# Five stage borders reordered, and the layer 0 cross attention issued in pairs of key tiles, in a four-layer decoder kernel

## The reference

```python
xn = layer_norm(x, g1, b1)                  # the context, 2 x 77 rows
ln_lat = layer_norm(latents, g2, b2)        # x after its own LayerNorm, 2 x 1024 rows
q = ln_lat @ Wq                             # 16 heads of 64
k, v = split(concatenate([xn, ln_lat], axis=1) @ Wkv)
weight = where(full_mask, einsum('bhld,bhnd->bhln', q * scale, k * scale), neg)
out = softmax(weight) @ v                   # 1024 queries, 1024 + 77 keys per item and head
return out @ Wout

x = x + L0_attn(_layernorm(x))          # gated scan
x = x + L0_xattn(ctx_1024, _layernorm(x), ...)      # as above
x = x + L0_ffn(_layernorm(x))           # integer weights, 256 -> 1024 -> 256
x = x + L1_attn(_layernorm(x))          # linear attention with two decays
x = x + L1_xattn(ctx_1024, ctx_1024, _layernorm(x));  x = x + L1_ffn(_layernorm(x))   # 8 experts
x = x + L2_attn(_layernorm(x))          # linear attention: 16 heads of 16, LayerNorm behind it
x = x + L2_xattn(...);  x = x + L2_ffn(...);  x = x + L3_attn(...);  x = x + L3_xattn(...);  x = x + L3_ffn(...)
```

## Time and profile before

| | us |
|---|---|
| median of 3 runs | 3242.64 (3238.62 to 3245.68) |
| the profiled execution's own time | 3243.5 |
| its span in the trace | 3241.8 |
| PE busy | 2901.1 (89%) |
| DVE busy | 1949.8 (60%) |
| ACT busy | 1456.5 (45%) |
| POOL busy | 1210.1 (37%) |
| mean granted TensorE clock | 0.943 |

### The profile page before, as it was taken

How to read it: one execution, slowest core, us unless ns; L and a number is a source line. 1 busy time by engine, 2 the same in 40 slices (tenths; PEclk the granted TensorE clock), 3 DMA queues, 4 the chain that set the end, 5 groups by cost and what they waited for, 6 DMA issues and landing times. The chain is left out here.

```text
span 3241.8 us, 48893 instructions
## 1 busy us (share of the span) xinstructions
PE 2901.1 (89%) x18490; PEld 1956.2 (60%) x18490; DVE 1949.8 (60%) x3101; ACT 1456.5 (45%) x2394; POOL 1210.1 (37%) x1001
## 2 busy tenths in 40 slices
PE   7869999999999979999998695999687888899977
PEld 6745555555555548888884564999465565344355
DVE  6556676676676754224218774555447858666576
ACT  3334444444444434324324373777333635355664
POOL 0026666666666640000004341566133403122232
PEclk9979999999999989999998896999798999799989
DMA  1100000000000002111101005666300000000010
GB/s 59 49 7 1 1 1 1 1 1 1 1 1 1 1 19 62 46 33 59 46 14 33 22 2 181 205 202 195 71 1 16 5 10 1 2 1 1 1 33 27
DMA packets 117131, 114.51 MB, mean 35 GB/s; under 512 B 22827, under 2 KB 102726, under 8 KB 116902
## 3 DMA queue, kind: packets, MB, share of 16 engines
q1 hardware_dynamic: 103173, 97.66, 9.7%
q0 software_dynamic: 7488, 9.48, 1.6%
q10 hardware_dynamic: 6240, 4.26, 0.4%
HBM read 100.81 MB, written 11.47 MB: 35 GB/s over the span
## 5 line engine op out<-in xcount | busy, mean ns | idle before, releaser
L827 POOL TENSOR_TENSOR acc<-acc,pf 128x512 f32<-128x512 f32 (+1 forms) x448 | 570.8, 1297 | 206.7 <-ACT pf L952 206.7
L1009 DVE TENSOR_REDUCE mxa<-ps 128x1 f32<-128x512 f32 x512 | 329.3, 684 | 290.3 <-PE ps L873 290.0
L952 ACT ACTIVATE pf<-ps 128x512 f32<-128x512 f32 x512 | 277.9, 595 | 278.0 <-PE ps L848 253.7
L861 PE MATMUL ps<-pf,v 128*64 128x512 f32 (+1 forms) x1152 | 311.7, 620 | 0.0
L3737 ACT ACTIVATE pT<-ps 128x1024 f32<-128x1024 f32 (+1 forms) x192 | 154.1, 811 | 134.3 <-PE ps L3654 133.8
L1204 POOL TENSOR_TENSOR x<-x,ys 128x256 f32<-128x256 f32 x16 | 11.8, 739 | 510.5 <-DVE ys L1409 510.5
L3750 DVE TENSOR_REDUCE mx<-ps 128x2 f32<-128x1024 f32 (+1 forms) x192 | 175.1, 951 | 45.4 <-PE ps L3641 37.4
L1858 POOL TENSOR_TENSOR e<-e,sm 128x1232 f32<-128x1232 f32 x48 | 107.9, 2247 | 168.3 <-DVE sm L2128 168.3
L2588 DVE TENSOR_TENSOR w_lo<-w2a,w_hi 128x2048 fp32r<-128x2048 f32 x39 | 89.4, 2292 | 101.5 <-ACT w_hi L2475 101.5
L2387 PE MATMUL ps<-xT,w1r 128*128 128x128 f32 x1248 | 148.2, 278 | 0.0
L2387 PEld LDWEIGHTS ps<-xT,w1r 128*128 128x128 f32 x1248 | 144.9, 195 | 0.0
(11 more groups left out here) (550 smaller groups left out, 7380.5 us busy)
## 6 DMA issues: line engine op xcount, KB each, us to landing
w1r<-in_f_w SPq DMA_DIRECT2D x39, 1024.0 KB, 5.1
w_raw<-in_c_h SPq DMA_DIRECT2D x32, 512.0 KB, 4.3
w2a<-in_f_w SPq DMA_DIRECT2D x8, 1024.0 KB, 13.0
w_raw<-in_c_w SPq DMA_DIRECT2D x32, 128.0 KB, 2.3
x<-in_x SPq DMA_DIRECT2D x1, 2048.0 KB, 8.2
moe_rows<-rowbuf ACTq DMA_DIRECT2D x4, 512.0 KB, 8.2
moe_acc<-x ACTq DMA_DIRECT2D x1, 2048.0 KB, 9.5
x<-moe_acc SPq DMA_DIRECT2D x4, 512.0 KB, 5.5
```

Of the source, the lines that this page charges most:

```text
L827: pool.tensor_tensor(now[0:r, :], now[0:r, :], pf[0:r, n % RING, a, :], ALU.add).then_inc(added.sem, 1)
L861: ins = pe.matmul(g.bk(3)[SIDE[a], :], v[0:r, u // 2 % 2, t, u % 2 * P + a * HD:u % 2 * P + (a + 1) * HD], pf[0:r, n % RING, a, :], start= ...
L952: act.activation(pf[0:r, n % RING, a, :], g.bk(bk.bank[f"s{n}_{a}"])[0:r, :], ACT.Exp, bias=bias)\
L1009: dve.tensor_reduce(mxa[:, q % 2, half, a, j:j + 1], g.bk(4 + a), AXX, ALU.max).then_inc(bk.release(f"m{q}_{i}_{a}"), 1)
```

## The change

Six parts, cut to the core. In the profile of the changed kernel the lines of the cross attention read: scores L862 and L859, values L872, maxima L884 and L888, sums L899, turn L909, v L916, k and q L925; DVE maxima L1035, lower halves L1065, reciprocal L1079, negation L1049 to L1055. The tile ws there also names the room of the probabilities.

**Into the cross attention.** The attention stage loads the 12 weight blocks and makes wH; its tail makes the statistics of x tiles 0 to 11. ScalarE writes both zH and zf from PSUM; VectorE no longer rounds.

```diff
+                for grp in range(4):
+                    for i, src in enumerate(nsrc):
+                        load(sp, nraw[:, grp, i], rows(src[grp]), next_in[grp])
...
+                        if f == 2:
+                            act.wait_ge(*next_in[c].at(0, 16 * len(nsrc)))
+                            act.activation(nH[:, c], nraw[:, c], ACT.Copy).then_inc(nH_made.sem, 1)
+                for n in (2, 3):
+                    root_scalar(g, act, 0, EARLY, spread, rooted, n)
...
-                added(NC - 1)
+                dve.wait_ge(*bk.read(f"y1_{NC - 2}", 0))
+                rows_vector(g, dve, 0, EARLY, spread, link)
+                inverse_vector(g, dve, 0, EARLY, rooted, 2, link)
+                variance_twice(g, dve, 0, EARLY, spread, link)
+                added(NC - 1, (0,))
+                inverse_twice(g, dve, 0, EARLY, rooted, 3, link)
+                added(NC - 1, (1,))
...
+                    normal(range(0, TC))
+                    for t in range(EARLY, NT):
+                        dve.bn_stats(bn[:, t - EARLY, :], g.x[:, t, :])
+                    normal(range(TC, 2 * TC))
...
-                        act.activation(wH[:, grp], ws[:, grp], ACT.Copy).then_inc(wH_made.sem, 1)
+                            src, how = g.bk(bk.bank[f"t{k}_{c}"])[:, 0:w], dict(scale=cols[:, at, k:k + 1], bias=cols[:, at + 1, k:k + 1])
+                            act.activation(zH[:, k, c0:c0 + w], src, ACT.Identity, **how).then_inc(zH_made.sem, 1)
+                            act.activation(zf[:, k, c0:c0 + w], src, ACT.Identity, **how).then_inc(bk.release(f"t{k}_{c}"), 1)
+                        if c < 2:
+                            roots(c)
```

```diff
-        TURN_AT, SUMS_AT, SCALE_AT, Y_AT, REC_AT = 6, 1, 4, (5, 7), {2: (0, 1), 3: (2, 3)}
-        QUERY_AT, KEYS_AT = 0, {2: 0, 3: 1, 4: 2}
-        VALUES_AT = {(0, 2): 0, (0, 3): 1, (0, 4): 2, (1, 2): 3, (1, 3): 4}
+        TURN_AT, SUMS_AT, SCALE_AT, Y_AT, REC_AT = 5, 0, 4, (6, 8), {1: (0, 1), 2: (2,), 3: (3,)}
+        QUERY_AT, KEYS_AT = 2, {1: 0, 3: 1, 4: 2}
+        VALUES_AT = {(0, 1): 0, (0, 3): 1, (0, 4): 2, (1, 1): 3, (1, 3): 4}
         VALUE_STEPS = 5
         KCOLS = [(0, CH), (CH, CH), (S, LP)]
 
-        MAXIMA_AT = {0: (1, 2), 1: (1, 3), 2: (1, 4), 3: (1, 5), 4: (1, 6), 5: (1, 7), 6: (2, 8), 7: (2, 0), 8: (2, 1)}
-        NEGATED_AT = 5
+        MAXIMA_AT = {0: (1, 4), 1: (1, 6), 2: (1, 5), 3: (1, 7), 4: (2, 0), 5: (2, 2), 6: (2, 1), 7: (2, 3), 8: (2, 8)}
+        NEGATED_AT = 3
 
...
-        fills = [(misc[o], 6 + i % 2) for i, o in enumerate(others)]
-        fills += [(f"s{n}_{a}", (2 * n + a) % 3) for n in range(Q * NT9) for a in range(HN)] + [(f"o{q}", 3) for q in range(Q)]
-        fills += [(f"m{q}_{i}_{a}", 4 + a) for q, i in items for a in range(HN)]
+        fills = [(misc[o], i % 4 if i < len(opened + between) else 7) for i, o in enumerate(others)]
+        fills += [(f"s{n}_{a}", 2 * (n % 2) + a) for n in range(Q * NT9) for a in range(HN)] + [(f"o{q}", 4) for q in range(Q)]
+        fills += [(f"m{q}_{i}_{a}", 5 + a) for q, i in items for a in range(HN)]
         bk = Banks(g, fills)
...
+                for n in range(0, Q * NT9, 2):
+                    for k in (n + 2, n + 3):
+                        if k < Q * NT9:
+                            scores(k)
+                    for m in maxima_in(*divmod(n, NT9)):
                         maxima(*m)
+                    for o in others_in(*divmod(n, NT9)):
+                        other(*o)
                     values(n)
-                    for o in others_in(q, t):
+                    if n % NT9 != NK:
+                        values(n + 1)
+                    for o in others_in(*divmod(n + 1, NT9)):
                         other(*o)
+                    if n % NT9 == NK:
+                        values(n + 1)
+                    for m in maxima_in(*divmod(n + 1, NT9)):
+                        maxima(*m)
                 for o in tail:
...
-                    for m in maxima_in(q, t):
-                        maxima(*m)
-                    if n:
-                        for o in others_in(*divmod(n - 1, NT9)):
-                            other(*o)
+                    if n % 2 == 0:
+                        for m in maxima_in(q, t):
+                            maxima(*m)
+                    for o in others_in(q, t):
+                        other(*o)
+                    if n % 2:
+                        for m in maxima_in(q, t):
+                            maxima(*m)
```

```diff
+                dve.wait_ge(*bk.read(misc["y", Q - 2, 1], 0))
+                rows_vector(g, dve, 0, EARLY, spread, link)
                 for part in range(TC):
                     invert(Q - 1, part)
                 scale(Q - 1)
-                for o in tail:
+                for o in tail[:-1]:
                     other(*o)
+                inverse_vector(g, dve, 0, EARLY, rooted, 1, link)
+                other(*tail[-1])
                 link.close()
...
-        def load_first(sp):
-            for m in range(RAW):
-                block_load(sp, m)
-            for dst, src in ((c1, s1), (c2, s2), (c3, hs1), (c4, hs2), (r3, s3)):
-                load(sp, dst[:], src, c_in)
-
-        ln_block(g, load_first)
```

```diff
+                        if HT <= t <= EARLY + 1:
+                            done = range(2 * (t - HT), min(2 * (t - HT) + 2, EARLY))
+                            if done and t <= EARLY:
+                                moments(g, dve, done)
+                            if t == EARLY + 1:
+                                link(moments(g, dve, (10, 11)))
+                                variance_vector(g, dve, 0, EARLY, spread, link)
...
+                def shifts(a, b):
+                    dve.scalar_tensor_tensor(shift[:, a:b], g.mean[:, a:b], -1.0, g.rstd[:, a:b], ALU.mult, ALU.mult).then_inc(shift_made.sem, 1)
+
+                shifts(0, EARLY)
                 dve.wait_ge(*none_made.at(0, 2))
                 for i in range(NI):
                     ins = dve.tensor_copy(summed[:, i, i * NH:(i + 1) * NH], hs[:].rearrange("p (h d) -> p h d", d=HD)[:, :, 0])
```

```diff
-        DONE, LEFT, FINISH_AT = 8, 3, {12: (0, 1), 13: (2,), 14: (3,), 15: (4,), 16: (5,), 17: (6, 7)}
+        DONE, LEFT, FINISH_AT = 8, 3, {12: (0, 1), 13: (2, 3), 14: (4,), 15: (5,), 16: (6, 7)}
+        MOMENTS_AT = {14: (0, 1), 15: (2, 3), 16: (4, 5), 17: (6, 7)}
...
-                    sp.dma_start(brow[0:1, i, :].rearrange("o (f p) -> o f p", p=P), src.rearrange("p f -> f p").unsqueeze(0), allow_slow_non_contiguous=True)\
-                        .then_inc(b_in.sem, 16)
-                for dst, src in ((wk, Wk), (wq, Wq)):
-                    for k in range(KD):
-                        sp.dma_start(dst[:, k].rearrange("p (h d) -> p h d", d=HD),
-                                     rows(src)[:, k].rearrange("p (h e) -> p h e", e=2 * HD)[:, :, 0:HD]).then_inc(kq_in.sem, 16)
-                for dst, src in ((same, same_head), (cau, causal), (wv, rows(Wv)), (rv, bv), (wo, rows(Wo)), (ro, bo)):
+                    load(sp, bpad[:, i, :], src, b_in)
+                load(sp, wkr[:], rows(Wk), kq_in)
+                load(sp, wqr[:], rows(Wq), kq_in)
+                load(sp, same[:], same_head, b_in)
...
+                dve.wait_ge(*kq_in.at(0, 32))
+                for dst, src in ((wk, wkr), (wq, wqr)):
+                    dve.tensor_copy(dst[:].rearrange("p k (h d) -> p (k h) d", d=HD), src[:].rearrange("p k (h e) -> p (k h) e", e=2 * HD)[:, :, 0:HD])\
+                        .then_inc(closed.sem, 1)
...
+                    if j == NT:
                         link(ins)
+                    if j in MOMENTS_AT and j <= NT:
+                        moments(g, dve, MOMENTS_AT[j])
                 link(dve.bn_stats(g.bn[:, NT - 1, :], out[:, NT - 1, :]))
                 variance_vector(g, dve, DONE, NT, spread, link)
-                rows_vector(g, dve, 0, DONE, spread, link)
+                link(moments(g, dve, MOMENTS_AT[NT + 1]))
+                variance_vector(g, dve, 0, DONE, spread, link)
                 inverse_vector(g, dve, DONE, NT, rooted, 2, link)
```

More of the change, by code:

```diff
@@ L374, in stage_l0_attn @@
         g.ev_bn = g.ev("bn_stats_done", 1)
-        spread, rooted, step = g.ev("ln_variance", 1), g.ev("ln_root", 1), g.ev("dve_step", LN_LINKS + 3 + HB * NC)
+        spread, rooted, step = g.ev("ln_variance", 3), g.ev("ln_root", 3), g.ev("dve_step", LN_LINKS + LN_TWICE_LINKS + 3 + HB * NC)
+        next_in, nH_made = [g.ev(f"weights{grp}_loaded", 16 * len(nsrc)) for grp in range(4)], g.ev("wH_made", 4)
         squared, ms_rooted, scales_made = g.ev("mean_square", 2), g.ev("mean_square_root", 1), g.ev("grow_shift_made", 1)
@@ L537, in gates, with added @@
                     dve.tensor_tensor(yT[:, c % 2, f, :], sc[:, f, :], go[:, f, :], ALU.mult).then_inc(gated.sem, 1)
-                def added(c):
+                def added(c, halves=range(2)):
                     dve.wait_ge(*grown.at(0, c + 1))
```

(27 more changed lines are left out.)

251 lines of the change are left out of this document (124 added, 127 removed).

## The result

The changed kernel takes 3277.89 us in the median (3275.81 to 3279.22, 4 runs), against 3243.85 (3238.62 to 3245.68, 4 runs) of the kernel before on the same chip: ratio 1.0107, interval 1.009 to 1.0125. It is slower by 34 us, where 13 were forecast; 3277.89 stands at the upper end of the forecast's own range of 3240 to 3278. The profiled execution took 3278.5 us, its span is 3276.8.

What follows compares the result with a forecast made beforehand. TensorE was taken to bound the loop, and other engines the borders where it waits. Loop +33 (waits 74, shape changes -41), prologue +2.6 and borders -21 gave 3257 us, own range 3240 to 3278 (overall 3195 to 3280).

Steps and rivals of the forecast that it cites:

- (b): Turn in the loop: waits for the short key piece's bank, which VectorE reads late; 1.4 lost 16 times, 23 us.
- Changes of shape: TensorE in the loop: a pair of tiles goes through shape changes once instead of twice; 46 saved, 5 added, net -41.
- the -36: Loop's net if, by the Trainium skill, each of 100 added changes of tiling mode drains TensorE.
- (a): Loop, maxima behind a k or q projection: VectorE does the lower half first; .66 lost 45 times, 30 us.
- (c): Loop's other halves: negation and reciprocal stand ahead of two maxima; 1.9 in each of 8 halves, 15 us.
- (d): Loop: sums wait for the bank until y is added behind the masked maxima; some .4, 14 times, 6 us.
- R3: Rival, slower: short waits in the loop lower the granted clock to a mean of .95, adding some 50 us: 3307; chance .08.
- the forecast case: Main case: loop +33, prologue +2.6, borders -21, giving 3257 us; chance .44.
- The prologue: Ahead of the loop's step 0: two more slices of maxima on VectorE, +2.6 us; four banks may give 1 back.
- The borders: Five stretches between stages where TensorE stands still: together -21 us (-38 to 0).
- Into the FFN: Border to the layer 0 FFN: 5.32 us go, 4.0 stand ahead of the last inversions; -1 (-5 to +4).
- the start of the layer 2 attention: Border: whole-row loads and two VectorE copies free the turn, -8; own and parity moved, -2; -10 (-12 to -5).

Runs made afterwards that it cites:

- e9: e5 with VectorE adding y before the masked maxima at step 8 of a half; 3174.52 us, ratio .9782 to the kernel before.
- e5: Changed kernel with the negation as one reduction and VectorE taking maxima ahead of lower halves in odd steps too; 3183.63 us, ratio .9810 to before.
- e8: e5 with four unused reductions on VectorE ahead of the negation in every even half, to make the turn late again; 3225.33 us, ratio .9932 to before.
- e7: Changed kernel with only the negation's third instruction removed, ScalarE turning the sign; 3240.59 us, ratio .9990 to before.

## Why the prediction was wrong

The sign was right, and so was the list of places at which TensorE would wait; the size was not: +34 us against +13. Two terms of the sum failed, the turn (b) and, bigger, the clock, which the sum put at nothing. By its steps:

- **Changes of shape.** Forecast -41 (46 less, 5 more); e9 shows some 45. The 5 for about 100 added changes had no ground. The orders printed above the prediction hold, for two steps with a projection in each, six changes before (maxima to values, values to projection, projection to scores, twice) and four after (maxima to projection, projection to values, values to projection, projection to maxima). So two go for each pair, with a projection or without, and the -36 worked out beside it counts changes that aren't added.
- **(a) Maxima behind a projection.** Forecast 45 × .66 = 30. In the trace after, the second matmul pair of such a maxima starts late (616.45 to 617.38 is .93, against .33 without a wait, and the first is some .05 late as well); it is so in 45 places, .66 each in nearly all of them, and e5 got 26.7 back. Right.
- **(b) The turn: here the prediction failed first.** Its step was the 1.5 to 2.5 us for the negation, priced from L1023 at .17 and L1024 at 1.14, which leaves the third instruction almost free. After, it took 3.0 to 3.2 us at the long turns, because the same change had put GpSimd's additions into runs of 4.95 us, and all three waited. The turn's idle came to 34 us (33.2 and 0.9) instead of 23. No row in front of the prediction shows the third instruction or a negation of 2.5 us, which (c) uses too; in the trace of before the third took over 1 us once in 32 times, and the three together 1.5 to 2.4 us in all halves but the first two. The Trainium skill would have told it (SBUF — State Buffer, Who interferes with whom): it lists `tensor_scalar` among the operations that can, under conditions, enter a mode with both ports and then contend with GpSimd, and says that `tensor_reduce` never does. The trace agrees on both: 1.20 for the `tensor_scalar`, .18 for the reduction in the same place.
- **(c) The other halves.** 15 forecast, 1.9 in each of 8 places. The trace has eight maxima ahead of a turn that cost 1.49 each in the mean, 12 us. One of them, of the changed kernel (.42 late at its start, .6 between its two pairs):

```profile
329.26 1.00 PE L884 MATMUL ps<-kH,qH 64*128 64x512 f32 x2 [0.31 <-DVE mxa L1035]
330.19 0.66 PE L909 MATMUL ps<-ident,nm 128*128 128x128 f32 x4
```

- **(d)** 6 forecast, 5.5 measured.
- **R3, the clock,** was a rival at .08 with a price of 50 us for the whole loop, and stood at nothing in the forecast case. It came inside the forecast case, in a smaller form: 17 us, nearly all behind the long turns (and 10 in e8). The error was to make it an alternative to the waits, though it comes with them: e7, whose turns wait 1.0 us, lost 1.7, and not behind a turn.
- **The prologue**: +2.6 forecast, +2.3 measured.
- **The borders**: -21 forecast, -18 measured. Into the cross attention it was -7.3 instead of -4: VectorE's busy time in the block fell from 33.12 to 23.74 us, so part of the rounding may have been a gain as well, which no run separates. Into the FFN -0.8, with the last inversions behind 12 statistics as forecast. At the start of the layer 2 attention it was -6.4 instead of -10: the turned z came, but the bias then waited for a load, and the eight key projections ran at a lower clock. Of the changed kernel, TensorE:

```profile
2350.51 1.94 PE L2800 MATMUL ps<-ident,z 128*128 128x128 f32 x8 [19.60 <-DVE z L2992]
2353.97 0.39 PE L2887 MATMUL ps<-bpad,pick 128*64 128x8 f32 x4 [1.52 <-DMA same<-in_same_head]
2354.51 6.60 PE L2804 MATMUL ps<-zT,wk 128*128 128x512 f32 x8 [0.16 <-DVE wq L3006]
2368.77 1.03 PE L2818 MATMUL ps<-q,kz 32*128 32x128 f32 x12 [4.22 <-DVE q L3020]
```

  Those eight took 5.00 us before and 6.60 now; the granted clock over them was .72 before and .55 now. At the end of the layer 2 attention nothing of the 1.5 us is left by the end of the span.

With 3.1 us for the negation the forecast's own chain for the turn gives 8.1 less 5.9, that is 2.2, and the trace has 2.26. From e9's loop without waits, 910.3, to the changed kernel's 1011.1 are 100.8 us: 30 (a), 34 (b), 12 (c), 5.5 (d) and 17 for the clock make 98.5. Some 2 us are not placed. The forecast had 74 there and 41 on the other side, where 50 came. So two errors of opposite sign stand in its result: 27 us too little for the waits and the clock, and 9 too little for the gain. That the total came out only 21 us off is in part luck.

Of the signs that it named, first scores 10 us closer and a loop of 975 to 995 us were missed (6.4 and, in its window, 1002.6). L1050 at 1 us or more came, and the turn's 1 to 2 us became 2.26. The .6 to .7 us ahead of L884 came too, but between the two pairs of the maxima, where the profile counts it as busy; so TensorE's idle is 48 us and not 60 to 80.

Two small slips in its sums change nothing: 1.4 × 16 is 22, not 23, and the borders' bounds add up to -39.

## What to carry to other kernels

When work is bunched on one engine, ask which short instructions on its neighbour will now stand behind it: an instruction of .17 us became one of 1.20, and three in a row became 3.1. Price a wait in a full loop twice, once as idle and once as what the clock may take behind it: here 15 long turns cost 33 us of idle and 15 us of clock, while waits of 1.0 us in the same place (e7) cost 15 us of idle and no clock behind them. And before a regrouping is given up, look at which single wait eats it: here the pairs were worth 50 us of the loop, and one reduction in place of three instructions and two swaps in VectorE's order turned a kernel 1% slower into one 2.2% faster.
